# Softmax denominators of an attention: two accumulating DMAs take over part of the partial sums, the totals work on 128 columns, and the output product is moved

## What is computed

```python
x = x + attention(layernorm(x))        # x: 1 x 2048 x 128, float32
# attention, 8 heads, inner width 128, latent width 32
c_q, c_kv = h @ W_DQ + b_DQ, h @ W_DKV + b_DKV
q = concat(c_q @ W_UQ + b_UQ, c_q @ W_QR + b_QR)      # per head
k = concat(c_kv @ W_UK + b_UK, h @ W_KR + b_KR)
attn = softmax(q @ k.T / sqrt(160))
o = attn @ (c_kv @ W_UV + b_UV)
return o @ W_O + b_O
```

## Time and profile before

| | us |
|---|---|
| median of three runs | 742.48 |
| lowest run | 739.45 |
| highest run | 1796.3 |
| span of the profiled execution | 737.8 |
| PE busy in it | 718.6 (97%) |
| DVE busy | 629.4 (85%) |
| POOL busy | 583.5 (79%) |
| ACT busy | 466.1 (63%) |

### The profile page before, as it was taken

The page is one execution under the profiler, slowest core; times in us unless marked ns, Lnnn a source line. Parts: engine busy times, 40 slices in busy tenths (PEclk is TensorE's granted clock), DMA queues, the critical chain, the costliest instruction groups (busy, mean ns, idle before and its releaser), DMA issues.

```text
span 737.8 us, 12518 instructions
## 1 busy us (share of the span) xinstructions
PE 718.6 (97%) x4180; PEld 469.0 (64%) x4180; DVE 629.4 (85%) x1304; ACT 466.1 (63%) x1069; POOL 583.5 (79%) x484
## 2 busy tenths in 40 slices
PE   8999999999999999999999999999899999999997
PEld 7665655655656656556556555466666699778885
DVE  8889999999999999999999899765978736878885
ACT  4367766766767767767667676654777831455553
POOL 6489989999999999999989999963689861446774
PEclk9999999999999999999999999999999999999999
DMA  6300000000000000000000000012000000032431
GB/s 148 91 1 2 1 2 2 2 3 2 1 2 2 1 2 3 1 1 2 2 1 3 2 1 2 2 46 74 2 1 0 2 1 1 1 87 74 141 103 28
DMA packets 40679, 15.57 MB, mean 21 GB/s; under 512 B 27292, under 2 KB 36525, under 8 KB 40616
## 3 DMA queue, kind: packets, MB, share of 16 engines
q1 hardware_dynamic: 39336, 14.67, 8.2%
q10 hardware_dynamic: 1280, 0.12, 0.1%
HBM read 13.35 MB, written 1.10 MB: 20 GB/s over the span
## 4 chain that ended last, share of the span: by engine, by line
PE 74%; POOL 11%; issue 7%; DVE 6%; ACT 1%; DMA 0%; POOLq 0%; DVEq 0%
PE ps L1482 17%; PE ps L1468 16%; PE ps L1526 15%; POOL hid_lo L1007 5%; PE ps L1510 4%; PE ps L1880 4%; PE ps L1537 3%; POOL nrm L987 2%; DVE mx L1061 2%; PE ps L1920 2%; PE ps L1922 1%; PE ps L1921 1%; POOL hid L987 1%; PE ps L1455 1%; PE ps L1456 1%
## 5 line engine op out<-in xcount | busy, mean ns | idle before, releaser
L1061 DVE TENSOR_REDUCE mx<-ps 128x1 f32<-128x512 f32 x492 | 302.6, 681 | 14.7 <-PE ps L1468 13.2
L622 ACT ACTIVATE prob<-ps 128x512 f32<-128x512 f32 x512 | 262.7, 630 | 9.2 <-PE ps L1482 9.1
L1482 PE MATMUL ps<-q_cols,key 128*128 128x512 f32 x512 | 209.5, 412 | 0.8 <-ACT prob L622 0.8
L1468 PE MATMUL ps<-key,q_rows 128*128 128x512 f32 x512 | 204.7, 404 | 0.8 <-DVE key L1047 0.4
L901 POOL TENSOR_TENSOR part<-part,prob 128x512 f32<-128x512 f32 x124 | 158.6, 1290 | 30.4 <-DVE part L1076 25.9
L1482 PEld LDWEIGHTS ps<-q_cols,key 128*128 128x128 f32 x512 | 95.4, 187 | 89.5 <-issue 50.7
L1526 PE MATMUL ps<-prob,val 128*32 128x512 f32 x1024 | 124.1, 598 | 0.0
L1468 PEld LDWEIGHTS ps<-key,q_rows 128*128 128x128 f32 x512 | 95.6, 188 | 23.0 <-DVE mx L1061 5.5
L901 POOL TENSOR_TENSOR part<-part,pair 128x512 f32<-128x512 f32 x64 | 95.9, 1499 | 0.1
L1007 POOL TENSOR_TENSOR hid_lo<-hid,hid_hi 128x512 fp32r<-128x512 f32 x44 | 61.5, 1410 | 38.6 <-ACT hid_hi L785 38.6
L901 POOL TENSOR_TENSOR pair<-prob 128x512 f32<-128x512 f32 x64 | 82.7, 1293 | 1.9 <-ACT prob L622 1.8
(11 more groups left out here) (285 smaller groups left out, 1172.6 us busy)
## 6 DMA issues: line engine op xcount, KB each, us to landing
g_all<-g_rows SPq DMA_DIRECT2D x9, 256.0 KB, 3.3
den<-den_sb SPq DMA_DIRECT2D x124, 2.0 KB, 2.1
g_all<-g_rows SPq DMA_DIRECT2D x6, 224.0 KB, 3.0
X<-in_L_attn_h_t_dram SPq DMA_DIRECT2D x4, 256.0 KB, 4.5
out_dram<-X SPq DMA_DIRECT2D x4, 256.0 KB, 2.4
g_all<-g_rows SPq DMA_DIRECT2D x6, 128.0 KB, 3.1
g_all<-g_rows SPq DMA_DIRECT2D x4, 192.0 KB, 3.6
w_raw<-in_L_ffn_w_g_dram SPq DMA_DIRECT2D x1, 704.0 KB, 4.5
```

Of the source, the lines that this page charges most:

```text
L622: act.activation(prob[:, g % RING, :], ps[:, g % 3, :], ACT.Exp, scale=SCALE).then_inc(s_exp, 1)
L1061: dve.tensor_reduce(mx[:, n % 2, c % TPB, at:at + 1], ps[:, BANK["rows", 2 * lin + j], :], AX.X, ALU.max).then_inc(s_mrd, 1)
L1468: pe.matmul(ps[:, BANK["rows", 2 * lin + j], :], q_rows[:, k, i * P:(i + 1) * P], key[:, h % KBUF, c0:c0 + BLK], start=True, stop=True).th ...
L1482: pe.matmul(ps[:, g % 3, :], key[:, n // NB % KBUF, t * P:(t + 1) * P], q_cols[:, n % NB, :], start=True, stop=True).then_inc(s_sc, 1)
```

## The change

Per block of keys, the sums are made in another way. POOL adds tiles 0+1, 2+3, 4+5, 6+7 into the four partial sums. One accumulating DMA, issued by POOL, adds the tiles 8 to 11 onto the four (1 MB read, `late_sums`). DVE adds 12+13 and 14+15 into `pair` (slot 7, and slot 0 of the next block). In the next block POOL adds `part[0]`, `part[2]` and the two pairs in one instruction of 128 x 1024 into `fin` (`add_pairs`), and a second accumulating DMA of 512 KB adds `part[1]`, `part[3]` onto it (`join_parts`). The totals are then eight matmuls of 128 columns, two for each quarter of the 512 queries, and come at slot 1 two blocks later. The copy, the spreading DMAs and `den` get a quarter of the size, and the reduce over four goes away. The output and the residual update go from slot 1 to slot 6; around the last two blocks the order is written anew. Two semaphores are merged with others.

```diff
+        def begun(n):
+            return 4 if n == 0 else 5 * n + 4
+        def paired(n):
+            return 5 * n + 7
...
-        def SUMS_AT(n):
-            return 6 if n < NBLK - 2 else 4
+        SUMS_AT, OUT_AT = 1, 6
...
-                if slot == 1 and 2 <= n < NBLK - 1:
-                    todo.append(("out", n - 2))
-                if slot == SUMS_AT(n) and 1 <= n < NBLK - 1:
-                    todo.append(("sums", n - 1))
-                if slot == 7 and n == NBLK - 2:
-                    todo.append(("out", n - 1))
+                if slot == SUMS_AT and 2 <= n < NBLK - 1:
+                    todo.append(("sums", n - 2))
+                if slot == OUT_AT and 2 <= n < NBLK - 1:
+                    todo.append(("out", n - 2))
...
+        fin = w_v[:, :, :].rearrange("p (x h) d -> p x (h d)", x=TPB)[:, 0:2, :]
...
-                            sp.dma_start(den[:, n % 2, g, :], den_sb[C * g:C * g + 1, :].rearrange("a (p i) -> a p i", i=TPB)).then_inc(s_dend, 16)
+                            sp.dma_start(den[C * g:C * (g + 1), n % 2, :],
+                                         den_sb[C * g:C * g + 1, 0:P].rearrange("a (p i) -> a p i", i=TPB)).then_inc(s_dend, 16)
...
-                        act.copy(den_sb[:, :], ps[:, BANK["sums", n], :]).then_inc(s_densb, 1)
+                        act.copy(den_sb[:, 0:P], ps[:, BANK["sums", n], 0:P]).then_inc(s_densb, 1)
...
-                        act.wait_ge(s_sum, ADDS * (n - 1) + 5)
-                    elif g >= RING and t == NT // 2:
+                        act.wait_ge(s_sum, begun(n - 1))
+                    elif g >= RING and t == 2 * NG:
                         act.wait_ge(s_pv, NW * n)
-                        act.wait_ge(s_sum, ADDS * n)
+                        act.wait_ge(s_late, 16 * n)
+                    elif g >= RING and t == 3 * NG:
+                        act.wait_ge(s_pair, 2 * n)
...
-                        if t == (2 * SUMS_AT(n) + 2 if n < NBLK - 1 else 8) and n >= 1:
+                        if t == 2 * SUMS_AT + 2 and n >= 2:
+                            sums_out(n - 2)
+                        if t == 10 and n == NBLK - 1:
                             sums_out(n - 1)
...
+                def begin_sum(n, g):
+                    if n >= 2 and g == 0:
+                        pool.wait_ge(s_join, 16 * (n - 1))
+                    ready(n, 2 * g + 1)
+                    pool.tensor_tensor(part[:, n % 2, g, :], tiles(n, 2 * g, 1)[:, 0, :], tiles(n, 2 * g + 1, 1)[:, 0, :], ALU.add).then_inc(s_sum, 1)
+                def late_sums(n):
+                    ready(n, 3 * NG - 1)
+                    pool.wait_ge(s_sum, begun(n))
+                    pool.dma_start(part[:, n % 2, :, :], tiles(n, 2 * NG, NG), accum_op=ALU.add).then_inc(s_late, 16)
+                def add_pairs(n):
+                    pool.wait_ge(s_late, 16 * (n + 1))
+                    pool.wait_ge(s_pair, 2 * (n + 1))
+                    if n >= 1:
+                        pool.wait_ge(s_ones, n)
+                    pool.tensor_tensor(fin, part[:, n % 2, bass.ds(0, 2, step=2), :], pair[:, :, :], ALU.add).then_inc(s_sum, 1)
+                def join_parts(n):
+                    pool.wait_ge(s_sum, paired(n))
+                    pool.dma_start(fin, part[:, n % 2, bass.ds(1, 2, step=2), :], accum_op=ALU.add).then_inc(s_join, 16)
+                for n in range(NBLK):
+                    begin_sum(n, 0)
...
+                    begin_sum(n, 1)
+                    if n >= 1:
+                        add_pairs(n - 1)
+                    begin_sum(n, 2)
+                    if n >= 1:
+                        join_parts(n - 1)
+                    begin_sum(n, 3)
+                    if n < NBLK - 1:
+                        late_sums(n)
...
+                def add_pair(n, j):
+                    t = NT * n + 3 * NG + 2 * j
+                    if n >= 1:
+                        dve.wait_ge(s_sum, paired(n - 1))
                     dve.wait_ge(s_exp, t + 2)
+                    dve.tensor_tensor(pair[:, j, :], prob[:, t % RING, :], prob[:, (t + 1) % RING, :], ALU.add).then_inc(s_pair, 1)
...
+                        if slot == 0 and n >= 1:
+                            add_pair(n - 1, 1)
...
-                            begin_sum(n, VSUM[0])
-                        if slot == 6 and n < NBLK - 1:
-                            begin_sum(n, VSUM[1])
+                        if slot == OUT_AT and 2 <= n < NBLK - 1:
+                            denominators(n - 2)
+                            accumulate(n - 2)
+                        if slot == 7 and n < NBLK - 1:
+                            add_pair(n, 0)
...
                     bank_read(("sums", n))
-                    pe.wait_ge(s_sum, ADDS * (n + 1))
-                    for g in range(NG):
-                        last = pe.matmul(ps[C * g:C * (g + 1), BANK["sums", n], :], ones_v[:, :], part[:, n % 2, g, :], start=True, stop=True)
+                    pe.wait_ge(s_join, 16 * (n + 1))
+                    parts = [fin[:, g, :] for g in range(2)]
+                    for g, of in enumerate(parts):
+                        for x in range(NG):
+                            last = pe.matmul(ps[C * x:C * (x + 1), BANK["sums", n], 0:P], ones_v[:, :], of[:, x * P:(x + 1) * P],
+                                             start=(g == 0), stop=(g == len(parts) - 1))
...
+                        if slot == OUT_AT and 2 <= n < NBLK - 1:
+                            output(n - 2)
                         if slot == 6:
                             weighted(n, 0)
-                        if slot == 1 and 2 <= n < NBLK - 1:
-                            output(n - 2)
                         if slot == 1 and n >= 1:
                             weighted(n - 1, 1)
-                        if slot == SUMS_AT(n) and 1 <= n < NBLK - 1:
-                            totals(n - 1)
-                        if slot == 7 and n == NBLK - 2:
-                            output(n - 1)
+                        if slot == SUMS_AT and n >= 2:
+                            totals(n - 2)
                         if n == NBLK - 1:
-                            if slot == 3:
+                            if slot == 2:
+                                output(n - 2)
+                            elif slot == 4:
                                 totals(n - 1)
-                            elif slot == 4:
                                 bank_read(("norm", 0))
                                 ln0_pe(pe, 0, 3)
```

More of the change, by code:

```diff
@@ L891, in _, with tiles @@
                 add_bias(3)
+                def tiles(n, first, count):
+                    at = (NT * n + first) % RING
+                    return prob[:, at:at + count, :]
                 def ready(n, tile):
                     pool.wait_ge(s_exp, NT * n + tile + 1)
-                def summed(n, count):
-                    pool.wait_ge(s_sum, ADDS * n + count)
-                def add(out, a, b):
-                    pool.tensor_tensor(out, a, b, ALU.add).then_inc(s_sum, 1)
-                def first_sums(n):
-                    def tile(t):
-                        return prob[:, (NT * n + t) % RING, :]
-                    total = [part[:, n % 2, g, :] for g in range(2)]
-                    if n >= 2:
-                        pool.wait_ge(s_ones, n - 1)
-                    ready(n, 1)
-                    add(total[0], tile(0), tile(1))
-                    ready(n, 3)
-                    add(pair[:, 0, :], tile(2), tile(3))
+                def begin_sum(n, g):
[3 more added lines that the diff above has]
+                    pool.tensor_tensor(part[:, n % 2, g, :], tiles(n, 2 * g, 1)[:, 0, :], tiles(n, 2 * g + 1, 1)[:, 0, :], ALU.add).then_inc(s_sum, 1)
@@ L915, in first_sums @@
+                def join_parts(n):
[3 more added lines that the diff above has]
+                    begin_sum(n, 0)
                     if n < 2:
                         columns(n + 2)
-                    ready(n, 5)
-                    add(total[1], tile(4), tile(5))
-                    summed(n, 2)
-                    add(total[0], total[0], pair[:, 0, :])
@@ L921, in first_sums @@
-                    ready(n, 7)
-                    add(pair[:, 1, :], tile(6), tile(7))
-                def last_sums(n):
-                    def tile(t):
-                        return prob[:, (NT * n + t) % RING, :]
-                    total = [part[:, n % 2, g, :] for g in range(NG)]
-                    pool.wait_ge(s_sumd, len(VSUM) * n + 1)
-                    ready(n, 10)
-                    add(total[2], total[2], tile(10))
-                    summed(n, 5)
-                    add(total[1], total[1], pair[:, 1, :])
-                    ready(n, 11)
-                    summed(n, 6)
-                    add(total[2], total[2], tile(11))
-                    pool.wait_ge(s_sumd, len(VSUM) * n + 2)
-                    ready(n, 14)
-                    add(total[3], total[3], tile(14))
-                    ready(n, 15)
```

(20 more changed lines are left out.)

48 lines of the change are left out of this document (17 added, 31 removed).

## The result

| | before | after |
|---|---|---|
| median of the runs, us | 740.97 (4 runs) | 772.69 (4 runs, 771.87 to 774.35) |
| span of the profiled execution, us | 737.8 | 770.5 |

The ratio is taken over the fast runs, without the one of 1796.3 us, and is 1.0456, with the interval [1.0422, 1.049]. By the medians the change costs 32 us (33 without that run), where 4.4 were forecast.

A forecast was written before the change was run, and what follows sets the result against it. PE, without holes, sets the 13.89 us block period. Span 737.8 - 5.5 + 2.9 + 7 = 742.2; its 4.4 increase added to the median 742.48 gives 746.9 us. Own range 738 to 754; 8 in 10, 732 to 775.

The forecast's parts named there:

- The steady order: Block period with the output at slot 6: 0.14 + 0.06, about 0.2 us less; 0.19 x 29 blocks = 5.5 us gained.
- saves 0.14 at its entrance: PE's slot-6 float32 stretch: entering with the output takes 0.24 us, against 0.38 with the weighted half.
- one pair of tiles (0.6): DVE's list after the slot-6 stretch starts: adding one pair of tiles was taken as 0.6 us.
- The totals' 0.43: PE's totals as eight 128-column matmuls: 0.85 us could fall to 0.43, gaining 0 to 0.43 a block.
- The shift: Small SP DMA from nmx to q_cols, awaited by the next block's first score: delayed, 0.1 x 29 = 2.9 us cost.
- is issued when exponential 11 ends, about 314.5: POOL's transfer of tiles 8-11: issued 1.2 us ahead of the shift (315.7), its bytes moving throughout the shift's 1.9 us.
- 0.2 a block if it costs what it cost at 149.0: Upper bound on the shift's cost, from one landing of 2.7 us for which PE waited 0.2.
- Rival 1: Shift held up, stopping PE: each us over 0.6 slack costs 29 us; delay 1.5 gives 770; chance 0.24.
- POOL's loop: POOL's adds and two transfers per block: L + 6.2 us, fitting a 13.7 us period while L is under 7.5.
- L: Landing time of the accumulating 1 MB transfer of tiles 8-11: taken as 7 us, between 5.5 and 8.8.
- rival 2: POOL's loop binds, L over 7.5: at 8.8 it takes 15.0 us and the kernel 787; chance 0.12.
- The tail: Block 31: PE's totals of block 30 wait for both transfers, costing 7 us; ends 5.6 and 10.5.

The follow-up runs named there:

- the first experiment: Changed kernel with the join (part[1], part[3] onto fin) done by one POOL tensor_tensor instead of the second DMA; 785.08 us, ratio 1.0621.
- the 1 MB copy: Kernel before plus a plain 1 MB SBUF-to-SBUF copy per block 2 to 30, on ACT's queue at exponential 11; 748.34 us, ratio 1.0135.
- the 512 KB copy: Kernel before plus a plain 512 KB SBUF-to-SBUF copy per block, on ACT's queue at exponential 11; 737.96 us, ratio 1.0001.

## Why the prediction was wrong

**The steady order (-5.5): wrong sign.** It came out at +0.46 a block, 12.0 over blocks 3 to 28. The step that failed is "Starting it with the output instead of the weighted half saves 0.14 at its entrance". The 0.24 was read at slot 1, where the bank that the output takes had long been freed; at slot 6, behind DVE's run of eight maxima, it waits for the last of them, and the entrance took 0.60. Then "one pair of tiles (0.6)": a pair took 0.73 to 0.81 from its start to that of the next instruction, and two of them push the key remainder, and the bank behind it, to 9.4 after the start of the stretch. The experiments that move only the output, with no transfer (+1.1), and only the order inside slot 6, with both transfers (-0.35), show that most of this is order and not traffic. The totals' 0.43 was right, and as the prediction said, PE could not use it.

**The shift (+2.9): right mechanism, wrong transfer, mis-sized.** Measured: 13 us over blocks 4 to 28. The failed sentence is that the transfer of tiles 8-11 "is issued when exponential 11 ends, about 314.5". It isn't: POOL's wide add waits for the totals that read the one fin, everything behind it on POOL slides, and the transfer leaves after the shift, while the join, which the prediction never set beside the shift, lands on it. Of the bound "0.2 a block if it costs what it cost at 149.0" nothing held: ordinary blocks lost nothing, since the first score now stands 3.2 behind the issue and a last packet at up to 2.6 is in time, a slack of 1.2 over the 1.37 and not 0.6; every third or fourth block lost 1.6, and in seven of these eight join and instruction fetch met, by the times on one engine. The landing at 149.0 that the bound rests on was a fetch as well: in the kernel before, one of 8 KB begins 1.25 us after that issue, the shift's last eight packets begin at +1.8, and no large transfer is there. It said nothing of what a transfer costs. Rival 1 gave 770 for a delay of 1.5, which comes close to the 772.7 by luck, with a different sum: the delay of the ordinary blocks (median landing 3.0 for 1.9) was real but free, the stalls are half of its 26, and the order supplied the rest.

**POOL's loop.** L was 7.4 (7 taken) and the join 5.0 (4.5 taken); rival 2 did not bind in the changed kernel, and did in the first experiment, where one more wide add stood in the loop. The issues are dearer than those of SP's rows: 0.90 and 1.20.
The Trainium skill's rule (DMA: Bandwidth & Descriptors, "Anatomy of one DMA") had given an estimate of 4.4 for the 1 MB; the accumulating transfer took 7.4, so here the measurement decides.

**The tail (+7): right.** 8.1 measured, of which 5.83 is the wait for the join. The wide add's own wait for fin (1.12) and the join's 5.0 are the difference.

**The range.** 772.7 lies outside the forecast's own range (738 to 754) and on the last 3 us of that for 8 in 10 (732 to 775). But slower had a chance of 0.36 only, because each rival was weighed against one term of the sum. Two terms went wrong at once: with the order's +12 alone, or the shift's +13 alone, beside the tail's 8, the time would already have passed the 2% line (740.97 + 14.8). Two figures of the prediction don't follow from its own terms: a delay of 1.0 gives 746.9 - 2.9 + 12 = 756, under its 2% line and not 758, and the tail's ends, with the 0.7 taken off as in its 7, are 4.9 and 9.8 and not 5.6 and 10.5. Neither moves the forecast.

## What to carry to other kernels

When work is moved on an engine, carry the waits for banks with it: read what frees each bank at the new place, and don't take an entrance from the old one. A single buffer (fin) between three engines ties their orders together; list who overwrites it before placing any issue in time. And when a small transfer gates the main engine, keep large transfers from being in the DMA engines when it is issued; if they must be, take the sum of what lies ahead of it, with an instruction fetch added, and compare that with the slack. A small transfer whose turn comes as the large one begins is no better off: in block 4 the two mixed and it still ended at 3.57.

## What the runs showed of the hardware

- A small transfer waited for the data ahead of it on each DMA engine, even from another queue: last packet at +1.37 us with nothing ahead, at 2.1 to 2.75 with the join ahead (3.3 in block 30), at +5.63 with the 1 MB. So it was where the large transfer's packets began 0.64 us or more ahead of the small one's. Where they began 0.1 to 0.2 us ahead (block 4 of the changed kernel, block 3 with the weighted half first) the two took turns, about one 2 KB packet to one small one, and the last ended at 3.57 and, with a fetch beside it, 3.64. The prediction's picture of one packet a turn holds for the second case alone.
- An accumulating packet of 8 KB took 629 ns, a plain one of 8 KB in the 1 MB copy 331; one of 2 KB took 178 to 180 with the adding, 81 to 84 without. Adding while moving went at about half the rate.
- A 16 KB packet of an instruction fetch took mostly 0.9 to 1.4 us, in the changed kernel about 0.95. With no large transfer beside it, it moved the shift's last packet from 1.37 to 2.6 at most. In the kernel before and with the 512 KB copy only a weight load waited, 0.2 to 0.4 us; where the order left no slack PE waited up to 1.5. Between a large transfer and the shift a fetch stopped PE for 1.6 in the changed kernel.
- A two-input add on DVE took 0.68 us alone and up to 2.25 beside POOL's two-input add of 128x1024; it is worth placing the two apart. The Trainium skill (SBUF — State Buffer, "SBUF: two separate sides") states this for a DVE operation with two SBUF inputs against a GpSimd operation that reads SBUF: the one that starts first holds the shared ports until it is done. The 0.57 above agrees.
